# When a product is done and where weights are split: three orders changed in a two-layer transformer kernel

## The reference, cut to what matters

```
x = x + attention0(layernorm(x))          # 16 heads, causal softmax
x = x + experts0(layernorm(x))            # 8 experts, 2 of them per token, 256 -> 1024 -> 256, gelu
x = x + attention1(layernorm(x))          # below
x = x + experts1(layernorm(x))            # 64 experts, 8 of them per token, and 2 shared ones

attention1(x):
    y = layernorm(x) * w + b
    q, k = tanh(y Wq) pi/4, tanh(y Wk) pi/4            # one number per head and token, 16 heads
    V = y Wv                                           # 64 per head
    cKV, sKV = cumsum(cos k * V), cumsum(sin k * V)    # along the tokens
    cK, sK = cumsum(cos k), cumsum(sin k)
    heads = (cos q * cKV + sin q * sKV) / (cos q * cK + sin q * sK + 1e-6)
    x = x + heads Wo
    return x + gelu(layernorm(x) W1 + b1) W2 + b2
```

## Time and profile before

| | |
|---|---|
| three timed runs | 2934.06, 2935.47, 2935.59 us; median 2935.47 |
| the profiled execution, its own time | 2929.47 us |
| its span, first to last instruction | 2927.8 us |
| busy in the span | TensorE 2488.2 (85%), VectorE 1812.3 (62%), ScalarE 1349.9 (46%), GpSimd 814.5 (28%) |
| TensorE's granted clock, mean | 0.923 of full speed |
| first expert block, first product to last store issued | 823.22 to 1287.22 |
| second attention, its first instruction and its stage 0 | 1293.6 and 1355.68 |
| the same product (values of stage 3) in two groups of eight stages | 1571.60 and 1646.40, 74.8 us apart |
| stage 4 of that second group starts on VectorE | 1660.72 |

### The profile page before, as it was taken

One profiled execution on the slowest core, in us unless ns is written; L12 is line 12 of the kernel. 1 busy time (PEld: TensorE's weight loads), 2 busy tenths in 40 slices (PEclk: granted clock), 3 DMA queues, 4 the chain that ended last, 5 costly groups with the idle time before them and its releaser, 6 DMA issues. The chain is left out here.

```text
span 2927.8 us, 54578 instructions
## 1 busy us (share of the span) xinstructions
PE 2488.2 (85%) x20412; PEld 2261.1 (77%) x20412; DVE 1812.3 (62%) x3235; ACT 1349.9 (46%) x2053; POOL 814.5 (28%) x1194
## 2 busy tenths in 40 slices
PE   4888888885279999954577788869999999999999
PEld 3666777773179999953466667759999999999999
DVE  7555555546268888857888777826655544554544
ACT  1454554442057667733343444334445545445454
POOL 6445455502600000024566665540000000000000
PEclk8899999987589999976889989989999999999999
DMA  9992000000267767755655554514422222222222
GB/s 302 337 332 95 1 1 2 1 1 27 92 206 240 233 226 234 233 183 127 149 133 135 133 129 129 139 53 145 131 85 86 80 96 86 87 89 90 86 78 87
DMA packets 194350, 373.34 MB, mean 128 GB/s; under 512 B 28708, under 2 KB 104680, under 8 KB 193128
## 3 DMA queue, kind: packets, MB, share of 16 engines
q1 hardware_dynamic: 184792, 343.31, 38.0%
q0 software_dynamic: 9360, 27.27, 2.8%
HBM read 336.95 MB, written 100.66 MB: 149 GB/s over the span
## 5 line engine op out<-in xcount | busy, mean ns | idle before, releaser
L2304 DVE TENSOR_TENSOR e_h_lo<-e_h,e_h_hi 128x512 fp32r<-128x512 f32 x320 | 221.7, 693 | 300.8 <-ACT e_h_hi L2380 300.8
L2442 PE MATMUL e_h_ps<-e_yT_hi,e_w_hi 128*128 128x256 f32 x1280 | 362.1, 283 | 3.4 <-ACT e_h L2366 2.6
L2458 PE MATMUL e_y_ps<-e_w_hi,e_h_hi 128*128 128x256 f32 x1280 | 358.9, 280 | 2.3 <-DVE e_h_lo L2304 2.1
L2442 PE MATMUL e_h_ps<-e_yT_lo,e_w_hi 128*128 128x256 f32 x1280 | 358.0, 280 | 0.0
L2442 PE MATMUL e_h_ps<-e_yT_hi,e_w_lo 128*128 128x256 f32 x1280 | 357.9, 280 | 0.0
L2458 PE MATMUL e_y_ps<-e_w_hi,e_h_lo 128*128 128x256 f32 x1280 | 355.4, 278 | 0.0
L2458 PE MATMUL e_y_ps<-e_w_lo,e_h_hi 128*128 128x256 f32 x1280 | 355.3, 278 | 0.0
L2380 ACT ACTIVATE e_h_hi<-e_h 128x512 fp32r<-128x512 f32 x320 | 202.2, 632 | 277.1 <-DVE e_h L2299 220.6
L2366 ACT ACTIVATE e_h<-e_h_ps,e_b 128x512 f32<-128x512 f32 x320 | 219.2, 685 | 174.6 <-PE e_h_ps L2442 152.3
L2299 DVE TENSOR_TENSOR e_h<-e_h,e_spread 128x512 f32<-128x512 f32 x256 | 176.6, 690 | 133.8 <-ACT e_h L2366 132.6
L468 DVE TENSOR_REDUCE a_top<-a_ring 128x2 f32<-128x1024 f32 (+3 forms) x256 | 202.6, 818 | 86.9 <-PE a_ring L676 85.9
(11 more groups left out here) (363 smaller groups left out, 7015.4 us busy)
## 6 DMA issues: line engine op xcount, KB each, us to landing
e_w<-in_w SPq DMA_DIRECT2D x78, 1024.0 KB, 5.5
e_spread<-share_store SPq DMA_DIRECT2D x512, 128.0 KB, 2.8
a_keys<-rows_store SPq DMA_DIRECT2D x128, 256.0 KB, 5.1
a_queries<-rows_store SPq DMA_DIRECT2D x86, 256.0 KB, 4.8
a_running_hidden<-rows_store SPq DMA_DIRECT2D x42, 256.0 KB, 4.6
e_xs<-sorted_x SPq DMA_DIRECT2D x39, 256.0 KB, 5.3
sorted_y<-e_ys POOLq DMA_DIRECT2D x39, 256.0 KB, 5.4
e_stage_buf<-in_w_all SPq DMA_DIRECT2D x10, 512.0 KB, 3.5
```

Of the source, the lines that this page charges most:

```text
L2304: dve.tensor_tensor(h_parts[q % 2][1][:, :], h[:, q % 2, :], h_parts[q % 2][0][:, :], ALU.subtract).then_inc(h_lo.sem, h_lo.tick())
L2442: last = pe.matmul(h_ps[q % 2][:, cols], l, r, start=(m == 0), stop=(m == len(ops) - 1))
L2458: last = pe.matmul(y_ps[n][:, 0:D], h_parts[q % 2][a][:, n * P:(n + 1) * P], w2[b][:, c, :], start=(q == 0 and m == 0), stop=(q == CH - 1 ...
```

## The change

Three things, with the parts of the diff that matter.

**The product at once.** In the stages c = 1, 4, 6 and 7 VectorE does `weigh_queries(n, 1)` in the stage itself, right behind `sum_up(n, 1)`; in the other four it stays in the next stage.

```diff
+            LONG = (1, 4, 6, 7)
...
-                if 0 < n <= CHUNKS:
+                if 0 < n <= CHUNKS and (n - 1) % HC not in LONG:
                     weigh_queries(n - 1, 1)
...
                     sum_up(n, 1)
+                    if c in LONG:
+                        weigh_queries(n, 1)
```

```diff
         @block.sync                                   (route0_phase)
+            sp.wait_ge(mapped.sem, mapped.at(1))
+            e = sp.value_load(g.slot_expert[0:1, 0:1], min_val=0, max_val=E0 - 1)
+            sp.dma_start(g.w1[:, :, :], t["w1_0"][bass.ds(e, 1)]. ...
+            sp.dma_start(g.w2[:, :, :], t["w2_0"][bass.ds(e, 1)]. ...
...
-            dve.tensor_copy(g.slot_expert[:, :], over[:, :]).then_inc(route_step.sem, route_step.tick())
+            dve.tensor_copy(g.slot_expert[:, :], over[:, :]).then_inc(mapped.sem, mapped.tick())
...
+            dve.wait_ge(first_w1.sem, first_w1.at(16))
+            dve.tensor_copy(g.w1_first[0][:, :, :], g.w1[:, :, :]).then_inc(first_split.sem, first_split.tick())
+            dve.wait_ge(first_split.sem, first_split.at(1))
+            dve.tensor_tensor(g.w1_first[1][:, :, :], g.w1[:, :, :], g.w1_first[0][:, :, :],
+                              ALU.subtract).then_inc(first_split.sem, first_split.tick())
+            dve.wait_ge(first_split.sem, first_split.at(2))
...
+            act.wait_ge(first_w2.sem, first_w2.at(16))
+            act.activation(g.w2_first[:, :, :], g.w2[:, :, :], ACT.Copy)
...
         @block.sync                                   (experts0_phase)
-            load(sp, 0, 0, lambda what: None)
+            load(sp, 0, 0, lambda what: None, weights=False)
...
         @block.vector
-            dve.wait_ge(w1_loaded.sem, w1_loaded.at(0))
-            dve.tensor_copy(w1_parts[0][0][:, :, :], w1[:, :, :]).then_inc(w1_split.sem, 1)
-            dve.wait_ge(w1_split.sem, 1)
+            for k, sem in ((9, w1_split), (10, w2_hi)):
+                dve.memset(g.scratch[:, k:k + 1], 0.0).then_inc(sem.sem, sem.base)
             halves = [slice(m * F0 // 2, (m + 1) * F0 // 2) for m in range(2)]
-            for f in halves:
-                dve.tensor_tensor(w1_parts[0][1][:, :, f], w1[:, :, f], w1_parts[0][0][:, :, f],
-                                  ALU.subtract).then_inc(w1_split.sem, 1)
...
         @block.scalar
-            act.wait_ge(w2_loaded.sem, w2_loaded.at(0))
-            act.activation(w2_parts[0][0][:, :, :], w2[:, :, :], ACT.Copy).then_inc(w2_hi.sem, 1)
             act.wait_ge(x_transposed.sem, x_transposed.at(0))
```

```diff
             for m, (_, name, c, n) in enumerate(BIG):
+                if m == 2:
+                    sp.wait_ge(combined.sem, combined.at(2 * TB, 0))
                 sp.dma_start(raw(m, c, n), ...
...
             low_weights(0)
+            centre_of(0)
             combine(1, LEFT)
-            centre_of(0)
             combine(1, RIGHT)
```

More of the change, by code:

```diff
@@ L1070, in sig @@
             return Signal(ctx, nc, "e0_" + name, per_turn, base)
-        w1, w2 = sb("w1", [P, KC, F0]), sb("w2", [P, FC0, D])
-        w1_parts = [[sb(f"w1_{part}{k}", [P, KC, F0], F32R) for part in ("hi", "lo")] for k in range(2)]
-        w2_parts = [[sb(f"w2_{part}{k}", [P, FC0, D], F32R) for part in ("hi", "lo")] for k in range(2)]
+        w1, w2 = g.w1, g.w2
+        w1_parts = [g.w1_first, [sb(f"w1_{part}1", [P, KC, F0], F32R) for part in ("hi", "lo")]]
+        w2_parts = [[g.w2_first, sb("w2_lo0", [P, FC0, D], F32R)], [sb(f"w2_{part}1", [P, FC0, D], F32R) for part in ("hi", "lo")]]
         b1, b2 = [sb(f"b1_{k}", [P, FC0]) for k in range(2)], [sb(f"b2_{k}", [P, D]) for k in range(2)]
@@ L1105, in experts0_phase, with load @@
         rows_out = t["sorted_y"].rearrange("(s n p) d -> s p n d", p=P, n=ST)
-        def load(sp, slot, kn, free):
+        def load(sp, slot, kn, free, weights=True):
             e = sp.value_load(g.slot_expert[0:1, bass.ds(slot, 1)], min_val=0, max_val=E0 - 1)
@@ L1113, in load @@
             free("w1")
-            sp.dma_start(w1[:, :, :], t["w1_0"][bass.ds(e, 1)].rearrange("o (c p) f -> p (o c) f",
-                                                                         p=P)).then_inc(w1_loaded.sem, 16)
+            if weights:
+                sp.dma_start(w1[:, :, :], t["w1_0"][bass.ds(e, 1)].rearrange("o (c p) f -> p (o c) f",
+                                                                             p=P)).then_inc(w1_loaded.sem, 16)
             free("rest")
@@ L1119, in load @@
             free("w2")
[L1120 to L1121 removed]
+            if weights:
+                sp.dma_start(w2[:, :, :], t["w2_0"][bass.ds(e, 1)].rearrange("o (c p) d -> p (o c) d",
+                                                                             p=P)).then_inc(w2_loaded.sem, 16)
         def transpose_x(pe, kn):
@@ L2509, in build @@
             g.slot_block = room.enter_context(nc.sbuf_tensor("slot_block", [1, MAPPED], I32))
-            with ExitStack() as normed:
-                g.y = normed.enter_context(nc.sbuf_tensor("y0", [P, NT, D], F32))
-                route0_phase(nc, g, t)
-            experts0_phase(nc, g, t)
+            with ExitStack() as weights:
+                g.w1 = weights.enter_context(nc.sbuf_tensor("e0_w1", [P, KC, F0], F32))
+                g.w2 = weights.enter_context(nc.sbuf_tensor("e0_w2", [P, FC0, D], F32))
+                g.w1_first = [weights.enter_context(nc.sbuf_tensor(f"e0_w1_{part}0", [P, KC, F0], F32R)) for part in ("hi", "lo")]
+                g.w2_first = weights.enter_context(nc.sbuf_tensor("e0_w2_hi0", [P, FC0, D], F32R))
+                with ExitStack() as normed:
+                    g.y = normed.enter_context(nc.sbuf_tensor("y0", [P, NT, D], F32))
+                    route0_phase(nc, g, t)
+                experts0_phase(nc, g, t)
             attention1_phase(nc, g, t)
```

7 lines of the change are left out of this document (6 added, 1 removed).

## The result

| | before | after |
|---|---|---|
| median of 20 timed runs each | 2935.53 us (2927.01 to 2943.29) | 2942.63 us (2935.96 to 2948.49) |
| ratio, 95% interval | | 1.0025 (1.0017 to 1.0033) |
| the profiled execution, its own time | 2929.47 us | 2940.83 us |
| its span | 2927.8 us | 2939.2 us |
| TensorE's granted clock, mean | 0.923 | 0.920 |

The kernel became 7.3 us slower (5.0 to 9.7, by the ratio), just beyond what a measurement tells from no change. The forecast was 4.8 more. Behind the small sum stand two large parts of opposite sign, and both can be read from the trace.

A forecast was written before the change was run, and what follows sets the result against it. It took TensorE to bound the first expert block and a ring of waits the second attention. 17.2 (product at once) − 9.1 (prelude) − 3.3 (attention's start) = 4.8 us more, 2940.3 us; 8 in 10: 2924 to 2948.

The forecast's parts named there:

- it strikes in all six groups: Second attention, angles after stage 2's gap: half clock costs 2.2 us in each of six groups, 13.2 more.
- stages 4, 6 and 7 cost next to nothing: Second attention, later groups: stage 4's moved product costs nothing, stage 6's falls into a wait, 6 and 7 add 0.13 thrice.
- The prelude: First expert block: first slot's weights fetched and split under the router's scatters, 9.1 us less, from 6.1 to 9.6.
- I take 0.5: Router: VectorE's new work holds up the scatters by 0.5 us, from 0 to 3.5.
- scatters that take over 2 us beside the new cast: Router: sign of being wrong, a scatter over 2 us beside VectorE's cast of the first w1.
- The start of the attention: Second attention's start: three late weights loaded after the first group's combine, its centre computed earlier; 3.3 us less, 0 to 4.
- I take 2.8: Attention's start: first group's last gathered tile used 2.8 us after it was asked for, not 6.1; 3.3 us less.
- the likeliest case: Whole kernel: the forecast itself, 4.8 us more, 2940.3 us, with its own range 2934 to 2942.
- Rival 1: Second attention: half clock falls into slack, so the early product costs 4.0; all 8.4 less, 2927.1 us; chance 0.22.
- Rival 2: Second attention: freeing PSUM early saves some 3 us in each of four groups; all 20 less, 2915 us; chance 0.14.
- Rival 3: Second attention: half clock covers all angle work, 3.0 us lost in six groups; 9.6 more, 2945.1 us; chance 0.27.
- Rival 4: Ahead of the experts: GpSimd held up or loads late, nothing saved beyond the half; 9 more, 2944.5 us; chance 0.05.

The follow-up runs named there:

- Filling the gap: The kernel after, with 28 zero-matrix products on TensorE ahead of the angles in stage 2 of six groups: 2931.41 us, ratio 1.0017 to before.
- The two kernels with stage 1 at once, unfilled and filled: Unfilled: before plus stage 1's early product, ratio 1.0035. Filled: also early first-slot expert weights, moved attention loads and zero products in gaps, ratio 0.9967.
- the filled kernel before: The kernel before with 13, 5, 9 and 16 products with zeros in the four gaps of each group: 2926.43 us, ratio 0.9993.

## Why the prediction was right

**The product at once: right in mechanism; that the sum fits is in part luck.** Forecast 17.2, measured 17.9. All the signs it named are there: stage 2's values without a wait, one gap (8.51 for the forecast 8.3), angles at 0.50, groups of 78.2 us (77.5 or more). In the group of the table stage 3 grew by 2.5, for 2.2 of clock and the part of VectorE's delay that reaches it; at full clock 0.50 of it remained, so the clock's own share there is 2.0, for the forecast's 2.2. Filling the gap is what shows it. Two terms were off, in opposite directions.

The first is "it strikes in all six groups", 13.2 in sum. The two kernels with stage 1 at once, unfilled and filled, differ in stage 3 by 0.8, 2.0, 2.1, 2.4, 1.5 and −0.4 us in the six groups, 8.6 together: the forecast holds in the three groups in the middle, while in the last the gap was only 3.6 us. Besides, the very first and the last group of eight became 1.4 and 1.2 us shorter in the unfilled one, where the early release did pay. The second is the step by which stages 4, 6 and 7 cost next to nothing beside their share of the first group's 1.0: they cost 7.9 (4.1 to 12.0) in time and 5.6 in the profile. The wait for the denominators had room for only part of the moved product (2.03 us in before, 1.30 in after), and stage 0 pays for stage 7's; 2.0 of the 5.6 are the jump of one stage, which also comes without the product. The two misses cancel.

**The prelude: right, with the price of the scatters mis-sized.** 9.6 less was forecast, and the profiles with the early split have 2.69 to 2.73 us from the transposes to the first product, 9.6 less than the 12.33 of before. The other four profiles without it have 12.74 to 13.33, so the saving is 9.6 to 10.6. The step "I take 0.5" failed: it was 1.96, within the stated 0 to 3.5. The row taken as the nearest, the scatter beside eight scalings, was not it; the row at the far end, a GpSimd operation of 0.20 us that took 2.13 beside a subtraction, was the same kind of meeting. What decides is how long the VectorE instruction that is running still takes: 1.02 and 1.20 us here, while each of the eight scalings lasts about a third of a microsecond, and the scatter beside them lost 0.18. That fits, but no run tried short instructions against a long one. On the cast, the Trainium skill (SBUF — State Buffer, "Who interferes with whom") had it: by its rule a scatter should lose about what is left of the cast, 1.02 of its 1.23 us, and it lost 0.89. The Trainium skill infers in the same section that a subtraction of two SBUF operands doesn't hold up descriptors; the traces disagree, 2.02 and 2.37 us against 0.96, and the measurement decides. Of the signs of being wrong, "scatters that take over 2 us beside the new cast" was missed narrowly: 1.85 beside the cast, 2.02 beside the subtraction.

**The start of the attention: the step "I take 2.8" failed.** The hedge in the same paragraph came true instead: the second group's gathers were slowed by the moved loads as the first's had been. Forecast 3.3 less; from the attention's first instruction to stage 0 the seven profiles with this part have 60.8 to 62.6 us, mean 61.5, the six without it 61.9 to 62.7, mean 62.3: 0.9 less, inside 0 to 4 and too little for a timed run. The first group's last tile came 4.3 us after it was asked for, not 2.8.

**The sum.** 17.9 − 10.8 − 0.9 = 6.2, against 7.3 measured and 4.8 forecast. The measured 2942.63 lies just above the likeliest case's own range (2934 to 2942) and inside the 2924 to 2948. Scatters (1.5) and gathers (2.4) were taken too lightly; the timed prelude did 3 us better than its own profile explains, which is inside its interval. The first attention multiply, forecast some 12.5 us earlier, was 7.1 earlier in the first profile of after, which has the late ranks described at the end, and 12.8 in the second; but 3.8 of these 12.8 were already there at the first scatter, so the two parts gave 9.0. *Rival 1* (the clock doesn't reach the ring) is ruled out by stage 3. *Rival 2* (the early release pays) is true only of the very first and the last group. *Rival 3* (slow clock over all of the angle work) gave 9.6, about as near to the 7.3 as the forecast, but not by its mechanism: 4.9 us at 0.50 cost 2.0 in the group of the table, below its point of 2.4, which one group of six reached. *Rival 4* did not occur.

**Left open.** Why stage 4 jumps between 13.8 and 15.8 us in unfilled kernels (with all gaps filled it is 13.8 in every steady group), whether stages 6 and 7 or stage 4 make the 7.9, which was not tried one by one, and why the 8.6 us that the filled kernel before saved in its profile's ring are not in its times.

## What to carry to other kernels

Before a wait of TensorE is removed, ask what it waits for next. Here two waits became one, and the half clock that follows a wait moved from work that had room behind it to work that others wait for. In those groups the removal saved nothing, and the moved slow stretch cost 2 us in each. Where such a wait can't be removed, products with zeros into an open accumulation held the clock here (1.00 instead of 0.91 over a group), as long as they ended before the wait would have; in stages where the wait is shorter or missing they were plain delay, and holding one restart can leave the next one longer. Work of VectorE beside indirect DMAs that GpSimd issues has a price as well: a scatter lost what the running instruction still had to do. Whether the same work in several short instructions costs less was not tried. A load that is moved out of one group's way stands in the next one's: look for a stretch in which the queue is empty, not for a later one.

## What was not expected of the hardware

**Three waits for the ranks were long in some jobs.** The first profile of after has three waits that no part of the change explains. The timeline of it, and of the same kernel in the second job:

```profile
725.38 0.35 PE L1061 MATMUL r_rank_ps<-r_both,r_ones 128*128 128x8 bf16 x8
...
733.97 0.23 DVE L904 TENSOR_TENSOR r_rank<-r_rank_ps,r_head 128x64 f32<-128x64 f32 x1 [8.95 <-remote]
```

```profile
723.79 0.34 PE L1061 MATMUL r_rank_ps<-r_both,r_ones 128*128 128x8 bf16 x8
724.17 0.22 DVE L904 TENSOR_TENSOR r_rank<-r_rank_ps,r_head 128x64 f32<-128x64 f32 x1 [0.66 <-PE r_rank_ps L1061]
```

VectorE starts 8.6 us after the first of these eight products in the one and 0.4 us after it in the other, at three places; the scatters last 93.1 us instead of 85.5, 7.6 more. The same waits (8.5 to 10.3 us) are in all four profiles of the last two jobs and in none of the eight of the first two jobs, and the kernel before was itself at 2937.99 and 2933.79 us in those last jobs, at 2928.13 and 2928.53 in the first two. So it goes with the job or the chip, not with the change: after itself has it in one profile and not in the other. That the timed runs of those jobs have it too is suggested by before's medians there, 5.3 to 9.9 us above the others, and not shown; the profile names no engine for the release (`remote`), and what delays it stays open. 7.6 of the 11.4 us between the first two profiles come from nothing that the change did, and only ratios within a job are to be trusted.

**The granted clock was a cost in a kernel that is not bound by TensorE.** Between 1400 and 1900 TensorE was busy 78% of the time in the kernel before, and yet the group of stages 24 to 31 was 2.6 us shorter with 51 useless matmuls in it, and four such groups 9.1 us together.
